# A one-core language-model layer: a new order table, extra identity turns on TensorE, and three smaller moves behind the attention

## Chip, core and metric

The kernel runs on one core of a Trainium2 chip. The metric is device time in microseconds (us) of one execution. Five engines work side by side and meet through semaphores: TensorE (PE in the profile, PEld its weight loads), VectorE (DVE), ScalarE (ACT), GpSimd (POOL) and SyncE (SP, which here only issues DMAs).

## What is computed

Ids of 4 x 512 tokens are hashed into an embedding table (192 wide), layer-normed, and pass through one attention block and one mixture-of-experts block.

```
h = layernorm_affine(table rows of the ids)            # 2048 tokens x 192
h = h + attention(layernorm(h))                        # 12 heads of 16
#   attn = softmax(q k^T / 4);  out = (attn v) W + b
#   t = out / |out| by head;  sim = softmax(10 t t^T where >= 0)
#   result = (sim v) W + b
h = h + moe(layernorm(h))                              # 8 experts, top 2
#   y = gelu(x w1[e] + b1[e]) w2[e] + b2[e], weighted, added by token
```

## The kernel before

**Attention.** The four sequences ("blocks" 0 to 3) have three groups of four heads each, 12 groups in all. For each group TensorE makes 16 score tiles of 128x512 three times: `max_unit` (row maxima, read by VectorE), `exp_unit` (scores again, ScalarE takes the exponential) and `sim_unit` (the second attention; ScalarE takes the exponential, VectorE's `mask` clears what stands under one). `pv` multiplies by V into an accumulator, ScalarE's `save` copies it out, TensorE's `normalise` turns it by transposes, and VectorE divides. `o_transpose`, `proj_norm` and `proj_out` are the projections behind it. All of TensorE's results pass through a ring of six PSUM banks. `wait_consumed(k)` waits until bank user k was read.

**The order.** `schedule()` lists all steps. The table `PLACE` gives each kind of step its positions in one common order `EVENTS`. Each engine walks this one list and takes the steps that are its own, so the table sets the order of work of each engine, SP's and GpSimd's DMA issues too. It holds no times.

**Routing.** While the last sequence is in its second attention, the first 12 token tiles are routed: VectorE's `shift`, `choose`, `place`, `mark` and `rows0` to `rows2` (24 one-hot tiles, one after another), TensorE's `list0` to `list2` (24 narrow matmuls, one for each one-hot tile), VectorE's `finish` (writes `slot_token`, from which GpSimd gathers expert inputs), and `share`, which works out the weights of the two chosen experts. The last four tiles ("late") are routed inside the expert loop.

**Behind the attention.** TensorE runs `o_transpose` and `proj_out` of the last sequence. VectorE adds into H, makes `out_norm` and X2. TensorE turns gathered tokens (`turn`), runs the first expert layer of a block of 128 slots (`first_wide`, 12 instructions, then `first_narrow`), turns X2 for the gate (`turn_gate`, `late_gate`), and goes into the loop `over_pairs`: 39 blocks, two by two. `second_layer(j)` waits for the GELU of block j and, before this change, for `y_weighted` of block j-2. VectorE's `weigh_output` adds the bias into Y, waits for the scatters of earlier blocks to land, and multiplies by the weight. GpSimd scatters Y with an adding DMA. In its second, fourth and sixth call (blocks 1, 3 and 5) `weigh_output` does the late routing between bias and weight. Weights w2 are loaded by eight DMAs that SP issues once `normalise` of the last group has been turned.

`keep_clock(bank, n)` multiplies the identity by the identity n times into a bank that nobody reads; 50 of these turns (`MASK_TURNS`) stand ahead of `pv` of the last group's third tile already.

Of the kernel before, what the change touches and what calls it, by code (L numbers as in the profile page):

```python
# [32 lines left out]
CT = N // P  # L33
# [29 lines left out]
MASK_TURNS = 50  # L63
PEELED = EARLY
# [10 lines left out]
def schedule():  # L75
# [43 lines left out]
    for t, part in ((0, "shift"), (0.1, "exp"), (2, "choose"), (4.5, "count"), (6, "place"), (7.5, "mark"), (7.7, "tag"),  # L119
                    (10.6, "rows0"), (10.8, "rows1"), (11, "rows2"), (12, "list0"), (12.5, "list1"), (13, "list2"),  # L120
                    (14, "finish"), (14.2, "stage"), (19, "share")):
        at(e + t, 6, "route", part)
    at(GB * UG * (B - 1) + GB * UG + OFF_E + 7.9, 6, "route", "take")
    for g in range(NG):
# [30 lines left out]
        0, 10, 60, 179),  # L155
    ('embed_norm', 'moments'): (
        1, 16, 65, 207),
    ('embed_norm', 'rstd'): (
        2, 27, 72, 231),
    ('embed_norm', 'centre'): (  # L160
        3, 34, 82, 233),
    ('load_qk',): (
# [4 lines left out]
    ('embed_norm', 'affine'): (  # L167
        7, 37, 91, 245),
    ('attn_stats', 'stats'): (
        8, 38, 96, 260),  # L170
    ('attn_stats', 'moments'): (
        9, 41, 108, 266),
    ('attn_stats', 'rstd'): (
        11, 44, 148, 272),
    ('attn_norm',): (
        13, 45, 175, 341),
    ('x_transpose',): (
        14, 18, 53, 64, 205, 212, 350, 353),
    ('q_proj',): (
        24, 67, 218, 398),  # L180
    ('mid', 'q_proj'): (
        26, 74, 224, 420),
    ('k_proj',): (
        33, 71, 222, 413),
    ('c_proj',): (
        35, 80, 234, 424),
    ('mid', 'k_proj'): (
        36, 78, 226, 422),
    ('v_proj',): (
        39, 43, 84, 92, 242, 249, 509, 521),  # L190
    ('mid', 'c_proj'): (
        40, 89, 241, 432),
    ('max_unit',): (
# [9 lines left out]
    ('max_row',): (  # L203
        70, 115, 164, 216, 268, 326, 389, 489, 557, 650, 734, 819),
    ('exp_unit',): (
# [109 lines left out]
def unit(kind, *args):  # L315

    return UNIT[(kind, args)]
# [1331 lines left out]
```

## Time and profile before

| | us |
|---|---|
| median of 3 runs | 600.11 (595.86 to 603.89) |
| the profiled execution, its own time | 599.07 |
| its span, first to last instruction | 597.3 |
| TensorE busy | 527.5 |
| VectorE busy | 428.8 |
| ScalarE busy | 336.5 |
| GpSimd busy | 226.8 |

### The profile page before, as it was taken

To read this page: it belongs to the slowest core of one execution; us is meant where nothing else is said; L and a number is where in the kernel's file an instruction comes from. 1 tells how busy PE (TensorE), PEld (TensorE's weight loads), DVE (VectorE), ACT (ScalarE), POOL (GpSimd) and SP (SyncE) were. 2 spreads that over 40 slices of the span, in tenths; PEclk is the share of its full clock that TensorE was granted. 3 is DMA by queue.
4 is the path that set the end of the run, shared out by engine and by line. 5 is a ranking of instruction groups with operands and counts; after the bars stand their busy time and mean duration, and the time that the engine had idled before them with its cause. 6 is when DMAs were issued, how large, how long until landed. Compare 5 with 4: busy or idle time off the path is not lost.

```text
span 597.3 us, 11968 instructions
## 1 busy us (share of the span) xinstructions
PE 527.5 (88%) x3532; PEld 322.8 (54%) x3533; DVE 428.8 (72%) x927; ACT 336.5 (56%) x790; POOL 226.8 (38%) x282
## 2 busy tenths in 40 slices
PE   0548899999999999999997987879999999999991
PEld 0223333443344323534253333568998999999990
DVE  3579997989898999897679999965775444434420
ACT  1223676768797888788977876215332424433430
POOL 6891221426151341102322320032455665656442
PEclk9979899999999999999998999868999999999996
DMA  4271142146442345321222659195232343333321
GB/s 118 61 128 32 37 72 45 41 69 115 52 71 56 57 67 76 42 66 47 63 49 86 87 115 289 43 314 189 33 52 44 57 62 49 47 60 47 45 29 20
DMA packets 42252, 45.24 MB, mean 76 GB/s; under 512 B 10419, under 2 KB 37045, under 8 KB 42198
## 3 DMA queue, kind: packets, MB, share of 16 engines
q0 software_dynamic: 12864, 19.97, 19.8%
q1 hardware_dynamic: 29334, 24.62, 18.0%
q8 instruction: 26, 0.43, 0.3%
q14 instruction: 28, 0.23, 0.2%
HBM read 17.88 MB, written 7.70 MB: 43 GB/s over the span
## 4 chain that ended last, share of the span: by engine, by line
PE 63%; DVE 19%; issue 6%; POOL 5%; ACT 3%; DMA 2%; DVEq 0%; POOLq 0%; ACTq 0%
PE psum L1400 12%; PE psum L1541 11%; PE psum L1518 8%; DVE MX L1187 6%; PE psum L1461 5%; PE psum L1468 5%; PE psum L1453 5%; PE psum L1525 4%; PE psum L1490 4%; DVE arena L1201 3%; POOL H L668 3%; PE psum L1425 2%; PE psum L1437 2%; ACT arena L828 2%; DMA result<-T,slot_dest 1%
## 5 line engine op out<-in xcount | busy, mean ns | idle before, releaser
L828 ACT ACTIVATE arena<-psum 128x512 f32<-128x512 f32 x384 | 205.1, 615 | 42.5 <-PE psum L1468 21.3
L1187 DVE TENSOR_REDUCE MX<-psum 128x1 f32<-128x512 f32 x192 | 123.3, 681 | 12.1 <-PE psum L1453 11.3
L1201 DVE SCALAR_TENSOR_TENSOR arena<-arena 128x1024 f32<-128x1024 f32 x96 | 117.1, 1241 | 10.3 <-ACT arena L828 10.1
L1400 PE MATMUL psum<-arena 128*17 128x512 f32 x768 | 102.9, 608 | 4.5 <-DVE arena L1201 3.1
L730 POOL DMA_INDIRECT result<-T,slot_dest x39 | 64.8, 1662 | 62.3 <-DVE T L1317 60.1
L573 POOL DMA_DIRECT2D KS<-arena x72 | 36.9, 514 | 112.1 <-PE psum L1468 53.7
L1468 PE MATMUL psum<-KS,QS 96*128 96x512 bf16 x192 | 66.3, 388 | 1.0 <-ACT arena L828 0.9
L712 POOL DMA_INDIRECT xg_sb<-x_rows,slot_token x39 | 40.1, 1028 | 69.4 <-DVE slot_token L1122 38.0
L861 ACT ACTIVATE arena<-psum,b_sb 128x128 f32<-128x128 f32 x120 | 32.2, 398 | 58.4 <-PE psum L1525 58.4
L1453 PE MATMUL psum<-late_stacks,arena 96*128 96x512 bf16 x144 | 51.6, 400 | 11.0 <-DMA late_stacks<-arena 7.6
L1518 PE MATMUL psum<-O,arena 128*128 128x128 f32 x468 | 58.9, 284 | 2.0 <-DVE O L942 1.3
L1518 PEld LDWEIGHTS psum<-O,arena 128*128 128x128 f32 x468 | 57.7, 200 | 2.8 <-DVE O L942 2.0
L573 POOL DMA_DIRECT2D late_stacks<-arena x72 | 37.1, 519 | 46.6 <-PE psum L1461 46.2
L1461 PE MATMUL psum<-arena,late_stacks 98*128 98x512 bf16 x144 | 52.5, 386 | 0.5 <-DVE MX L1187 0.3
L861 ACT ACTIVATE SQ<-psum,b_sb 128x128 f32<-128x128 f32 x60 | 16.6, 376 | 53.4 <-PE psum L1525 53.4
L564 POOL TENSOR_TENSOR arena<-arena 128x512 bf16<-128x512 f32 x18 | 21.7, 1210 | 64.2 <-ACT arena L780 64.2
L938 DVE COPY arena<-arena 128x1152 f32 x39 | 30.5, 798 | 19.5 <-PE psum L1525 12.6
L1317 DVE TENSOR_SCALAR T<-T,X 128x192 f32<-128x192 f32 x39 | 12.5, 320 | 43.9 <-DMA result<-T,slot_dest 32.1
L1468 PEld LDWEIGHTS psum<-KS,QS 96*128 96x128 bf16 x192 | 17.6, 99 | 46.4 <-issue 29.4
L1541 PE MATMUL psum<-arena 128*128 x240 | 41.1, 327 | 1.0 <-DVE T L1317 0.7
L1541 PEld LDWEIGHTS psum<-arena 128*128 128x128 f32 x240 | 38.7, 190 | 1.6 <-issue 1.5
L1461 PEld LDWEIGHTS psum<-arena,late_stacks 98*128 98x128 bf16 x144 | 13.9, 98 | 38.0 <-issue 17.0
(223 smaller groups left out, 759.7 us busy)
## 6 DMA issues: line engine op xcount, KB each, us to landing
late_stacks<-arena POOLq DMA_DIRECT2D x72, 64.0 KB, 3.7
QS<-arena SPq DMA_DIRECT2D x72, 64.0 KB, 3.6
KS<-arena POOLq DMA_DIRECT2D x72, 64.0 KB, 3.8
arena<-w SPq DMA_DIRECT2D x8, 576.0 KB, 9.3
arena<-arena SPq DMA_DIRECT2D x54, 64.0 KB, 3.6
arena<-w SPq DMA_DIRECT2D x8, 384.0 KB, 7.6
x_rows<-X SPq DMA_DIRECT2D x4, 384.0 KB, 3.9
result<-H SPq DMA_DIRECT2D x4, 384.0 KB, 5.0
```

Of the source, the lines that this page charges most:

```text
L573: eng.dma_start(dst[g % SLOTS[ps]][r * D:(r + 1) * D, :, :].rearrange("d h n -> d (h n)"), part_rows(role, parts[r], g)).then_inc(done[g % ...
L730: pool.indirect_dma_start(out, bass.IndirectOffsetOnAxis(ap=slot_dest[:, j:j + 1], axis=0), Y[j % 2], None, compute_op=ALU.add).then_inc(s ...
L828: act.activation((P1, P2)[ps][:, n % PRING, :], s, ACT.Exp, scale=(QSCALE, SIM_SCALE)[ps]).then_inc(done, 1)
L861: last = act.activation(HT[r][:, hc, :], hid_ps[h][hc], ACT.Gelu, bias=b1_sb[:, bass.ds(e, 1), hc:hc + 1].rearrange("p o h -> p (o h)"))
L1187: dve.tensor_reduce(MX[:, g % 2, CT * i + c:CT * i + c + 1], slot(k), AX_X, ALU.max).then_inc(freed[k % RING], 1)
L1201: dve.scalar_tensor_tensor(p, p, 1.0, p, ALU.is_ge, ALU.mult).then_inc(masked, 1)
L1400: last = pe.matmul(acc[ps][32 * i:32 * i + VW, :], V[b][:, c, GH * (g % GB) + i, :], (P1, P2)[ps][:, n % PRING, :], start=c == 0, stop=c = ...
L1453: last = pe.matmul(s, QS[0][sl][0:SD, i, c * P:(c + 1) * P], KS[0][sl][0:SD, i, :], start=True, stop=True)
L1461: last = pe.matmul(s, KS[0][sl][:, i, c * P:(c + 1) * P], QS[0][sl][:, i, :], start=True, stop=True)
L1468: last = pe.matmul(s, QS[1][sl][:, i, c * P:(c + 1) * P], KS[1][sl][:, i, :], start=True, stop=True)
L1518: pe.matmul(hid_ps[i][hc], W1S[i][:, hc * P:(hc + 1) * P], XGT[i][:, 0, :], start=hc % HB == 0, stop=False, skip_group_check=True)
L1541: last = pe.matmul(y_ps[i], HT[r][:, hc, :], w2_sb[:, bass.ds(e, 1), hc, :].rearrange("p o d -> p (o d)"), start=hc == 0, stop=hc == HC - 1)
```

## The change

1. `PLACE` is a new table. The order within the last stage, from the third-last group on, moves by a few places; of 789 steps of TensorE 270 change their position in its own order, nearly all by one to four.
2. `share` of the early tokens goes from the end of the list, ahead of `stage(1, 1)`, to behind `stage(2, 0)` in VectorE's program ("behind block 1's tokens").
3. `second_layer(j)` waits for `y_biased` of block j-2, no longer for `y_weighted`.
4. The last block (38) gets a Y buffer of its own, so its bias goes ahead of the wait for the scatter of block 36.
5. Identity turns: one ahead of every second list matmul (12), seven ahead of the last `pv`, seven ahead of the last `normalise`, three ahead of the last `o_transpose`, seven ahead of the last `proj_out`, and seven each ahead of and behind `turn(0, 0)`.

```
@@ schedule @@
-                    (14, "finish"), (14.2, "stage"), (19, "share")):
+                    (14, "finish"), (14.2, "stage")):
@@ PLACE (most of the table left out) @@
     ('embed_norm', 'affine'): (
-        7, 37, 91, 245),
+        4, 25, 98, 240),
...
     ('save', 1): (
-        465, 571, 656, 737, 818, 877, 944, 980, 1017, 1059, 1101, 1138),
+        464, 568, 656, 736, 817, 878, 944, 981, 1022, 1068, 1102, 1138),
...
     ('out_norm', 'rstd'): (
-        735, 932, 1062, 1147),
+        726, 936, 1062, 1147),
...
     ('route',): (
-        1088, 1092, 1106, 1117, 1118, 1120, 1125, 1129, 1131, 1132, 1134, 1135, 1136, 1137, 1139, 1146, 1149),
+        1088, 1091, 1106, 1116, 1118, 1120, 1125, 1129, 1131, 1132, 1134, 1135, 1136, 1137, 1139, 1145),
@@ buffers, GpSimd @@
-        Y = [T[:, 2 + i, :] for i in range(2)]
+        Y = [T[:, 2 + i, :] for i in range(2)] + [T[:, 0, :]]
-  ... Y[j % 2], None,
+  ... Y[2 if j == NBLK - 1 else j % 2], None,
@@ VectorE, weigh_output @@
+                    last = isinstance(j, int) and j == NBLK - 1
+                    y = Y[2 if last else i]
                     dve.wait_ge(y_filled, j + 1)
-                    wait_past(dve, scattered[i], 8 * j0)
-                    dve.tensor_tensor(Y[i], y_ps[i], ...).then_inc(y_biased, 1)
+                    if not last:
+                        wait_past(dve, scattered[i], 8 * j0)
+                    dve.tensor_tensor(y, y_ps[i], ...).then_inc(y_biased, 1)
                     dve.wait_ge(y_biased, j + 1)
+                    if last:
+                        dve.wait_ge(scattered[i], 16 * (j // 2))
@@ VectorE, before the loop @@
                 stage(2, 0)
+                share(0)
@@ TensorE (GAP_TURNS = 7) @@
                             if args[0] == "list0":
+                                wait_consumed(pe, k + 1 - RING)
                                 pe.wait_ge(tags_ready, 2)
                                 pe.wait_ge(row_ready, n * EARLY_TILES + t + 1)
+                                if t % 2 == 0:
+                                    keep_clock(slot(k + 1), 1)
                                 last = pe.matmul(tokens_ps, oh_row[n][:, t, :], ...)
+                        if (g, c, ps) == (NG - 1, CT - 1, 1):      # last pv
+                            wait_consumed(pe, k + 1 - RING)
+                            keep_clock(slot(k + 1), GAP_TURNS)
+                            if args == (B - 1, 1, 0):              # last o_transpose
+                                keep_clock(s, GAP_TURNS // 2)
+                        if args == (NG - 1, 1):                    # last normalise
+                            keep_clock(s, GAP_TURNS)
+                        if (kind, *args) == ("proj_out", B - 1, 0):
+                            keep_clock(s, GAP_TURNS)
@@ second_layer @@
-                    wait_past(pe, y_weighted, j - 1)
+                    wait_past(pe, y_biased, j - 1)
@@ behind the list of steps @@
                     pe.wait_ge(acc_saved[ps], NG)
+                keep_clock(gate_ps[1], GAP_TURNS)
                 pe.wait_ge(tokens_ready, 1)
                 pe.wait_ge(lists_ready, 1)
                 turn(0, 0)
+                keep_clock(gate_ps[1], GAP_TURNS)
```

## Rows read from the trace of the kernel before

**Rows 1.** Busy time by stretch: PE, PEld, DVE, ACT, POOL, then PEclk, DMA share, GB/s.

```profile
380.00:390.00 10.00, 7.84 (x77) 5.31 (x76) 9.64 (x41) 1.70 (x3) 0.00 (x0) 1.00 0.10 28
500.00:550.00 50.00, 50.00 (x438) 48.66 (x438) 20.22 (x45) 19.27 (x72) 30.87 (x23) 1.00 0.33 52
```

**Rows 2.** The same view, 1 us each, where the granted clock changes.

```profile
391.00:392.00 1.00, 0.57 (x2) 0.60 (x3) 0.21 (x1) 0.29 (x1) 0.70 (x2) 0.70 1.09 348
...
405.00:406.00 1.00, 0.76 (x7) 0.51 (x5) 0.56 (x2) 1.00 (x5) 0.00 (x0) 0.97 1.08 354
...
411.00:412.00 1.00, 0.38 (x4) 0.28 (x3) 0.96 (x5) 0.99 (x2) 0.82 (x1) 0.94 0.03 10
```

**Rows 3.** The chain that ended last, 383 to 412: start, duration, what.

```profile
384.89 3.90 DVE late_stacks L1109 x24
...
391.43 5.47 PE psum L1490 x16
...
399.50 2.93 PE psum L1518 x12
...
406.28 1.60 PE psum L1518 x12
...
411.75 4.54 PE psum L1518 x24
```

**Rows 4.** TensorE in order of time: start, duration, line, operands, count, idle before.

```profile
66.68 0.39 PE L1453 MATMUL psum<-late_stacks,arena 96*128 96x512 bf16 x1 [1.68 <-DVE MX L1187]
...
348.39 1.47 PE L1490 MATMUL psum<-PW,OT 97*128 97x192 f32 x8
...
377.27 5.86 PE L1362 MATMUL psum<-ident 128*128 128x128 f32 x50
...
384.94 1.05 PE L1400 MATMUL psum<-arena 128*17 128x512 f32 x8 [0.83 <-DVE arena L1201]
386.81 0.63 PE L1479 MATMUL psum<-ident,arena 128*128 128x128 f32 x4 [0.81 <-ACT arena L788]
387.27 1.77 PE L1375 MATMUL psum<-arena,late_stacks 128*128 128x32 bf16 x24
389.56 1.05 PE L1425 MATMUL psum<-ident,O 128*96 128x128 f32 x8 [0.52 <-DVE O L1212]
...
398.01 0.45 PE L1510 MATMUL psum<-ident,xg_sb 128*128 128x128 f32 x1 [1.12 <-issue]
...
450.00 2.21 PE L1541 MATMUL psum<-arena,X 128*128 x12 [1.34 <-DVE T L1317]
...
452.05 2.84 PE L1518 MATMUL psum<-O,arena 128*128 128x128 f32 x24
```

**Rows 5.** VectorE in order of time.

```profile
400.34 1.25 DVE L923 TENSOR_SCALAR X<-H,mv,rstd_out 128x192 f32<-128x192 f32 x4
...
410.67 0.19 DVE L1339 COPY LG<-psum 128x32 f32<-128x32 f32 x1 [1.96 <-PE psum L1577]
...
451.01 0.75 DVE L942 COPY O<-psum 128x256 f32<-128x256 f32 x2
...
585.46 0.36 DVE L1308 TENSOR_TENSOR T<-psum,arena 128x192 f32<-128x192 f32 x1 [2.09 <-DMA result<-T,slot_dest]
586.66 0.32 DVE L1317 TENSOR_SCALAR T<-T,X 128x192 f32<-128x192 f32 x1 [0.85 <-DVE T L1308]
```

**Rows 6.** Busy time by stretch where VectorE runs `share` (columns of Rows 1).

```profile
401.50:403.90 2.40, 2.40 (x17) 2.00 (x15) 2.02 (x12) 0.00 (x0) 0.00 (x0) 0.50 1.12 334
```

**Rows 7.** First gather of expert inputs: issue on GpSimd, then time to landing.

```profile
390.19 1.05 POOL L712 DMA_INDIRECT xg_sb<-x_rows,slot_token  x1 [37.96 <-DVE slot_token L1122]
...
DMA to landing us min/median/max: 6.6/6.6/6.6
```

**Rows 8.** The eight loads of w2 on SP: durations, first and last start, landing.

```profile
L646 SPq DMA_DIRECT2D arena<-w x8: 373/1458/2490, 387.5 to 396.3; - x8
...
DMA to landing us min/median/max: 4.1/9.3/11.0
```

More of the change, by code:

```diff
@@ L63 @@
 MASK_TURNS = 50
+GAP_TURNS = 7
 PEELED = EARLY
@@ L154 @@
     ('embed_norm', 'stats'): (
-        0, 10, 60, 179),
+        0, 8, 59, 191),
     ('embed_norm', 'moments'): (
-        1, 16, 65, 207),
+        1, 11, 65, 212),
     ('embed_norm', 'rstd'): (
-        2, 27, 72, 231),
+        2, 12, 80, 230),
     ('embed_norm', 'centre'): (
-        3, 34, 82, 233),
-    ('load_qk',): (
[4 rows of a table removed]
-    ('embed_norm', 'affine'): (
-        7, 37, 91, 245),
[L169 to L178, printed above, removed]
+        3, 13, 82, 233),
+    ('embed_norm', 'affine'): (
+        4, 25, 98, 240),
+    ('attn_stats', 'stats'): (
+        5, 31, 103, 263),
+    ('attn_stats', 'moments'): (
+        6, 34, 123, 272),
+    ('attn_stats', 'rstd'): (
+        7, 35, 135, 285),
+    ('attn_norm',): (
+        9, 39, 169, 339),
+    ('x_transpose',): (
+        10, 14, 51, 60, 206, 211, 351, 353),
@@ L179 @@
+    ('load_qk',): (
[4 rows of a table added]
     ('q_proj',): (
-        24, 67, 218, 398),
+        17, 66, 218, 400),
     ('mid', 'q_proj'): (
-        26, 74, 224, 420),
+        19, 72, 224, 419),
     ('k_proj',): (
-        33, 71, 222, 413),
+        21, 71, 222, 410),
     ('c_proj',): (
-        35, 80, 234, 424),
+        23, 78, 234, 428),
     ('mid', 'k_proj'): (
-        36, 78, 226, 422),
+        26, 76, 226, 421),
+    ('mid', 'c_proj'): (
+        30, 87, 243, 430),
     ('v_proj',): (
-        39, 43, 84, 92, 242, 249, 509, 521),
@@ L191 @@
-    ('mid', 'c_proj'): (
-        40, 89, 241, 432),
+        37, 38, 84, 91, 237, 245, 509, 521),
     ('max_unit',): (
[9 rows of a table removed]
[9 rows of a table added]
     ('max_row',): (
-        70, 115, 164, 216, 268, 326, 389, 489, 557, 650, 734, 819),
+        70, 112, 162, 215, 268, 325, 390, 492, 560, 651, 733, 820),
     ('exp_unit',): (
[9 rows of a table removed]
[9 rows of a table added]
     ('pv', 0): (
[3 rows of a table removed]
[3 rows of a table added]
     ('save', 0): (
-        142, 191, 243, 298, 361, 439, 534, 614, 705, 782, 860, 915),
+        142, 188, 244, 296, 359, 439, 531, 626, 702, 781, 856, 911),
     ('normalise', 0): (
-        159, 198, 250, 312, 370, 446, 540, 631, 711, 803, 875, 917),
+        161, 199, 251, 313, 369, 446, 543, 632, 714, 803, 879, 917),
@@ L729, in _ @@
                     pool.wait_ge(y_weighted, j + 1)
-                    pool.indirect_dma_start(out, bass.IndirectOffsetOnAxis(ap=slot_dest[:, j:j + 1], axis=0), Y[j % 2], None,
+                    pool.indirect_dma_start(out, bass.IndirectOffsetOnAxis(ap=slot_dest[:, j:j + 1], axis=0), Y[2 if j == NBLK - 1 else j % 2], None,
                                             compute_op=ALU.add).then_inc(scattered[j % 2], 16)
@@ L1112, in _ @@
                             stage(0, 0)
-                        elif part == "share":
-                            share(0)
                         elif part == "take":
@@ L1304, in weigh_output @@
                 def weigh_output(j0, j, i, meanwhile=None):
+                    last = isinstance(j, int) and j == NBLK - 1
+                    y = Y[2 if last else i]
                     e = dve.value_load(blk_expert[0:1, bass.ds(j, 1)], min_val=0, max_val=E - 1)
                     dve.wait_ge(y_filled, j + 1)
[L1307 to L1308 removed]
+                    if not last:
+                        wait_past(dve, scattered[i], 8 * j0)
+                    dve.tensor_tensor(y, y_ps[i], b2_b[:, bass.ds(e, 1), :].rearrange("p o d -> p (o d)"), ALU.add).then_inc(y_biased, 1)
                     dve.wait_ge(y_biased, j + 1)
+                    if last:
+                        dve.wait_ge(scattered[i], 16 * (j // 2))
                     if meanwhile is not None:
@@ L1386, in _ @@
                         if (g, c, ps) == (NG - 1, CT - 2, 1):
-                            wait_consumed(pe, unit("normalise", NG - 1, 1) - RING)
-                            keep_clock(slot(unit("normalise", NG - 1, 1)), MASK_TURNS)
+                            wait_consumed(pe, k + 1 - RING)
+                            keep_clock(slot(k + 1), MASK_TURNS)
+                        if (g, c, ps) == (NG - 1, CT - 1, 1):
+                            wait_consumed(pe, k + 1 - RING)
+                            keep_clock(slot(k + 1), GAP_TURNS)
                         if ps == 0:
```

33 lines of the change are left out of this document (16 added, 17 removed), and 94 rows, old and new, of the table PLACE.

## Prediction

> **What bounds the kernel now.** I read the busy time by stretch first, for the clock and for the engine that is never idle, then the chain of waits, then TensorE and VectorE in order of time around each wait that the change touches. Three stretches come out. In the expert loop TensorE is the bound: busy 50.00 of 50 us, clock 1.00 [rows 1]. In the attention TensorE and VectorE share the chain, and the waits are short. Between them, from 384 to 412 us, neither is full: TensorE is busy 7.84 of the ten us from 380 [rows 1], and the chain goes from VectorE's one-hot tiles to `proj_out`, `out_norm`, and the first expert block [rows 3].
>
> In that third stretch the reader is to look at the clock. It falls at about 391.3, comes back just ahead of 405.0, and falls again close to the end of the slice from 411 [rows 2]. What TensorE did before the first fall was short work with waits between (0.83, 0.81, 0.52 us) and 24 list matmuls of 32 columns, and `proj_out` came next [rows 4]. The price stands in pairs of rows. The 16 instructions of `proj_out` took 5.47 us at 1.2 GHz [rows 3], and eight of the same kind 1.47 at 2.4 GHz [rows 4]. `first_wide` took 2.93 us for 12 at 1.2 GHz and 1.60 for 12 at 2.4 [rows 3]. After the second fall, 24 took 4.54 [rows 3], against 2.84 at full clock [rows 4]. So much for what the turns are after. By what they cost, one turn is 5.86 / 50 = 0.117 us [rows 4] at full clock.
>
> **Do turns hold the clock?** The 50 turns ran alone from 377.27 to 383.13 [rows 4], and the clock was 1.00 through the ten us from 380 [rows 1] and on to 391.3 [rows 2]. So they count as work by the trace. The Trainium skill, page "TensorE: Matmul & The Clock Gate", section "Part 4: PE-mode transpose", says the opposite: in transpose mode the full clock doesn't engage, since it isn't counted as a busy TensorE in the same way. By that rule the new turns are only cost; by the trace of before it doesn't hold here. It is the third case below. What the trace can't show is how many turns are enough.
>
> **The turns, followed in time.** Nothing changes up to the last `pv` but the table. Seven turns are 0.82 us and stand in the wait of 0.83 ahead of the last `pv`, and the next seven in the wait of 0.81 ahead of `normalise` [rows 4]: nothing for both.
>
> The 12 turns among the list matmuls are not hidden. VectorE made the 24 tiles from 384.89 in 3.90 us, 0.163 each [rows 3], so 14 lie ready when the lists start at 387.27, and TensorE works them off at 1.77 / 24 = 0.074 each [rows 4]. With a turn for each two, a pair takes 0.265, still under VectorE's 0.326, so TensorE lags to the end: 24 x 0.074 + 12 x 0.117 = 3.2 us, the lists end at 390.45, against 389.04. That is 1.4 us on two paths. First, three turns (0.35) and `o_transpose` follow: it starts at 390.8, not 389.56 [rows 4], 1.2 late. The seven turns ahead of `proj_out` fit its wait for ScalarE's copy (0.82, from the end of `o_transpose` to 391.43, rows above). So `proj_out` starts at 392.65 and takes two times about 1.43 = 2.85 at full clock: it ends at 395.5, against 396.9, **1.4 early**. Second, `finish` has its lists 1.4 later, so the first gather goes out at about 391.6, not 390.19, and lands 6.6 later [rows 7], at 398.2. Before, it landed at 396.8 and `turn(0, 0)` at 398.01 [rows 4] waited for other things. It now becomes the late one: VectorE's add and statistics are done by 397.3, the seven turns ahead of `turn(0, 0)` (ready at 396.0, done by 397) are hidden by the gather, and the turn, its copy and the first `first_wide` come at 398.2, 398.5 and 398.9, against 399.50 [rows 3]: **0.6 early**. The seven turns behind `turn(0, 0)` lie in the wait for that copy.
>
> Because the copy now goes ahead of the moments, and waits for the gather, X2 (done at 401.6 before [rows 5]) comes some 0.4 later, at 402.0. `first_wide` and `first_narrow` of block 0 at full clock are done by 401.4, so `turn_gate` waits for X2, and ends at about 403.2 with `turn(1, 1)`. `first_wide` of block 1 starts at 403.8, against 406.28 [rows 3], **2.5 early**. From there to the first wide layer of block 2 was 411.75 - 406.28 = 5.47 us at full clock [rows 3], and stays that, if VectorE follows.
>
> **`share`.** It takes 2.02 us of VectorE and some 2.3 with its gaps, from 401.50 to 403.83 [rows 6]. Before, it was covered by TensorE at half clock. With TensorE 2.5 early it would have been on the path in its old place (`stage(1, 1)`, then the copy of block 1's tokens). In the new place it falls into the idle 1.96 us in which VectorE waits for the late gate [rows 5]: 2.3 - 1.96 = 0.35 sticks out. So the loop begins 2.5 - 0.4 = **2.1 early**, at 409.65. The eight w2 loads are the transfer that could cap this. The last was issued at 396.3 and landed within 11.0 [rows 8], at 407.3 counted from its start: 2.3 us of slack.
>
> **The second fall** has its own price: 4.54 - 2.84 = 1.7 us. No turns stand in the stretch ahead of it (`late_gate` with 8 columns at a time). Its work doesn't change, but where it lies does, and ahead of it TensorE now runs at full clock and almost without a gap. I take it as avoided in the likelier case, since the fall came so near the end of that stretch, and price the other separately.
>
> **`y_biased`.** `second_layer(7)` waited 1.34 us until 450.00 for the weighing of block 5 [rows 4], behind `share` and the tags of the late tokens. That wait goes. What is late next is VectorE itself: the copies of blocks 8 and on for TensorE come out of its queue only behind that weighing, the first at 451.43 (451.01 and half of 0.75, plus the semaphore) [rows 5], while `first_wide` started at 452.05 [rows 4]. So **0.6** comes back, not 1.34. The chain of VectorE and scatter landings from 424 to 450 doesn't change.
>
> **Last block.** Its bias waited 2.09 us for block 36's scatter, ran at 585.46, and the product followed at 586.66 [rows 5]. Now the bias is done before, and the product follows the landing (about 585.4) by one register load and a semaphore, some 0.4: 585.8. **0.85** saved, all on the end. GpSimd's scatter only follows.
>
> **The table.** Start to 42 us: the first maxima wait for GpSimd's queue of loads, which the new order leaves alone up to group 0's last load; `mid` of `c_proj` goes eight places up on GpSimd, ahead of loads of group 1, which are used only after group 0's maxima. ScalarE's root of sequence 1 now goes ahead of the second `x_transpose`, which delays the projections a little while the loads wait for GpSimd anyway: nothing. At 66.68 TensorE waited 1.68 us [rows 4] for VectorE, which had `embed_norm` of sequence 2 ahead of three maxima; these now come first. The wait is shortened, but VectorE does the same work in all. In the last stage `out_norm` of sequence 2 has its root ahead of `save` of group 9 and of three exponentials: X2 comes a little earlier, and the exponentials behind it a little later. Bounds from the rows: from -1.7 (that wait wholly gone, nothing else) to +1.7 (as much lost by a swap elsewhere). I take -1.0, nearer the gain, as that row shows a wait that the new order goes around and no row shows one that it makes.
>
> **Sum, likeliest case.** Turns and `share` 2.1, second fall avoided 1.7, `y_biased` 0.6, last block 0.85, table 1.0: 6.25. The profiled execution took 599.07 us (span 597.3 and 1.8 around it), 1.0 under the median. Against the mean of the four executions shown, 599.73, it gives 593.5; against the profiled one 592.8.
>
> **Cases.**
> A, 0.42: as summed, 593.5.
> B, 0.25: the clock holds over the first stretch and falls over the second. 1.7 less: 595.2. For it: no turns there, and 8-column matmuls. Against: the stretch is short.
> C, 0.13, the other side: the turns don't hold the clock, by the rule quoted from the Trainium skill or because they are too few. Place: between 391 and 405. Price: `o_transpose` 1.2 late; `proj_out` at half clock as before; the turns ahead of `turn(0, 0)` at 0.234 each, 1.64 us, and now in series: it runs 2.8 late; the seven behind it exceed the wait by 0.8: the expert block starts 3.6 late. Less 0.6, 0.85 and 1.0 from the rest: 1.15 slower, 600.9. It decides when the clock falls before 392.6, where `proj_out` starts. Against: the 50 turns.
> D, 0.08: the table loses. If ScalarE's earlier root stalls the exponentials of group 10 behind it for over a us, and the swap of maxima costs a new fall of the clock (1.7 by the second fall's rows), the table costs 3 in place of giving 1: 597.5.
> E, 0.12: the table gives more: the wait at 66.68 and the half clock behind it (2 x 1.7), and waits of the last stage: 5 in place of 1, so 589.5.
>
> **Range.** It reaches from 588 (E and some luck of the runs) to 600.5 (C less a little); the three runs of before alone spread by 8. 2%, 12 us, is about what a measurement of this kernel can tell from no change. Faster by more than that (under 588.1) only in part of E: 0.09. Slower: 0.01. The same: 0.90.
>
> **What would show it.** Right: PEclk 1.00 from 378 through 405; `proj_out` 16 instructions in about 2.9 us; lists ending 1.4 later against the one-hot tiles; `turn(0, 0)` ended by the gather; `first_wide` of block 8 released by VectorE's copy, no idle at `second_layer`; the last bias directly behind TensorE. Wrong: 0.50 in `proj_out` (C), 0.50 ahead of the loop (B), a loop start set by w2 (then the 2.1 shrinks), or the end of the attention moved by more than 2 us (D, E).

## The result, and the profile after

The changed kernel took 599.09 us (median of 20 executions, 597.97 to 602.92), the kernel before 597.57 (20, 595.78 to 603.89): ratio 1.0043, interval [1.0028, 1.0059]. So it was slower by some 2.6 us by the ratio, where 6.25 less had been summed. In two later groups of runs the same changed kernel came out at 0.9973 [0.9941, 1.0004] and 1.0006 [0.9984, 1.0027] (below). What follows finds a gain behind the attention and a new table that gives it back; why the three ratios differ is only in part explained. Two executions of table_alone_again (below), its profiled one among them, were slow ones, over 1.5% longer than its fastest, and are left out of its ratio.

The profiled execution took 602.92 us (span 601.1). By stretch, 396 to 410 us, columns as in [rows 1]; these answer to [rows 1, 2]:

```profile
396.00:397.00 1.00, 0.94 (x8) 0.73 (x7) 0.53 (x3) 0.56 (x2) 0.69 (x2) 1.00 1.10 341
401.00:402.00 1.00, 0.47 (x5) 0.23 (x3) 0.40 (x2) 0.00 (x0) 0.00 (x0) 1.00 1.02 326
402.00:403.00 1.00, 0.00 (x0) 0.00 (x0) 0.00 (x0) 0.00 (x0) 0.00 (x0) 0.68 1.05 328
409.00:410.00 1.00, 1.00 (x13) 0.88 (x10) 0.00 (x0) 0.32 (x2) 0.00 (x0) 0.91 1.10 338
504.00:554.00 50.00, 50.00 (x438) 48.66 (x438) 20.22 (x45) 19.21 (x72) 30.84 (x23) 1.00 0.33 52
```

The expert loop is as it was. The clock now holds through `proj_out` and falls at 402.4, in a slice in which no engine works at all. TensorE in order of time says what they wait for (answers to [rows 3, 4, 7]):

```profile
396.71 2.85 PE L1507 MATMUL psum<-PW,OT 97*128 97x192 f32 x16
400.51 0.96 PE L1367 MATMUL psum<-ident 128*128 128x128 f32 x7 [0.95 <-issue]
403.42 0.45 PE L1527 MATMUL psum<-ident,xg_sb 128*128 128x128 f32 x1 [1.95 <-DMA xg_sb<-x_rows,slot_token]
...
403.87 1.70 PE L1367 MATMUL psum<-ident 128*128 128x128 f32 x7
405.37 2.77 PE L1535 MATMUL psum<-O,arena 128*128 128x128 f32 x12
...
411.27 1.60 PE L1535 MATMUL psum<-O,arena 128*128 128x128 f32 x12 [0.52 <-DVE O L943]
...
417.30 2.92 PE L1535 MATMUL psum<-O,arena 128*128 128x128 f32 x24 [1.19 <-issue]
...
440.75 4.07 PE L1558 MATMUL psum<-arena 128*128 x24
444.78 2.94 PE L1535 MATMUL psum<-O,arena 128*128 128x128 f32 x24
...
449.68 2.12 PE L1558 MATMUL psum<-arena,SQ 128*128 x12
451.64 2.11 PE L1558 MATMUL psum<-arena,X 128*128 x12
...
455.18 2.94 PE L1535 MATMUL psum<-O,arena 128*128 128x128 f32 x24 [1.43 <-DVE O L943]
```

`proj_out` took 2.85 us, as forecast, against 5.47. But the first turn of gathered tokens waits 1.95 us for the gather and starts 7.9 us after its issue, where the landing alone took 6.6 before [rows 7]. The clock falls in that wait, the seven turns behind it take 1.70 us and not 0.96, and `first_wide` of block 0 takes 2.77 us, hardly less than the 2.93 of before [rows 3]. At the end, VectorE (answers to [rows 5]):

```profile
588.30 0.36 DVE L1310 TENSOR_TENSOR T<-psum,arena 128x192 f32<-128x192 f32 x1 [0.43 <-PE psum L1558]
590.47 0.32 DVE L1321 TENSOR_SCALAR T<-T,X 128x192 f32<-128x192 f32 x1 [1.81 <-DMA result<-T,slot_dest]
```

The bias no longer waits, as meant. The product waits for the scatter of block 36 instead.

And the one-hot tiles, which began at 384.89 [rows 3], began at 389.74: 4.9 us late, when of the new turns only the seven ahead of the last `pv` had run. Part of that lies at the start. VectorE, ScalarE and GpSimd of the changed kernel, in order of time:

```profile
23.23 7.37 POOL L675 MEMSET late_stacks<- 2x2048 bf16 x4
...
23.78 0.18 DVE L913 BATCH_NORM_AGGREGATE mv_x<-stats_in 128x2 f32<-128x6 f32 x1 [0.62 <-issue]
25.20 0.18 DVE L913 BATCH_NORM_AGGREGATE mv_x<-stats_in 128x2 f32<-128x6 f32 x1 [1.25 <-issue]
25.91 0.18 DVE L913 BATCH_NORM_AGGREGATE mv_x<-stats_in 128x2 f32<-128x6 f32 x1 [0.52 <-issue]
26.12 0.30 ACT L745 ACTIVATE log_in<-mv_x,eps_embed 128x4 f32<-128x4 f32 x1 [2.63 <-DVE mv_x L913]
26.57 0.57 ACT L799 ACTIVATE arena<-psum 96x512 f32<-96x512 f32 x1
```

The same in the kernel before:

```profile
21.77 0.21 DVE L912 BATCH_NORM_AGGREGATE mv_x<-stats_in 128x2 f32<-128x6 f32 x2
22.39 0.59 ACT L798 ACTIVATE arena<-psum 96x512 f32<-96x512 f32 x1 [0.26 <-PE psum L1425]
```

The copy that lets the projections start (L799, L798 before) now stands on ScalarE behind the root of sequence 1, the root waits for VectorE's aggregates, and these crept. The projections began at 27.24, not 23.08, and the first maxima at 44.41, not 41.92 (both starts from TensorE in order of time). Of these 4.2 us 1.4 lie ahead of that root already: the eight transposes of the first `x_transpose` steps, which began at 20.44, began at 21.81. What made the 2.5 us at the first maxima 4.9 by the one-hot tiles was not traced.

### The profile page after: what moved, and what is told of

Read it like the earlier page. It is cut to its first block, busy times and chain, and to the rows that moved or that the text cites. A ratio compares the mean times of both kernels' runs of the same rounds, so it can differ in the third digit from the quotient of the medians.

```text
span 601.1 us, 12066 instructions
## 1 busy us (share of the span) xinstructions
PE 531.6 (88%) x3582; PEld 325.1 (54%) x3583; DVE 431.3 (72%) x927; ACT 335.1 (56%) x790; POOL 228.6 (38%) x282
## 4 chain that ended last, share of the span: by engine, by line
PE 59%; DVE 21%; issue 6%; DMA 5%; ACT 4%; POOL 1%; DVEq 1%; POOLq 0%; ACTq 0%
PE psum L1411 10%; PE psum L1558 10%; DVE MX L1186 8%; PE psum L1535 7%; PE psum L1474 5%; PE psum L1481 4%; PE psum L1466 4%; PE psum L1542 4%; PE psum L1450 3%; PE psum L1507 3%; DVE arena L1200 3%; ACT arena L829 3%; DMA result<-T,slot_dest 3%; PE psum L1438 2%; PE psum L1367 2%
## 5 line engine op out<-in xcount | busy, mean ns | idle before, releaser
L1535 PE MATMUL psum<-O,arena 128*128 128x128 f32 x468 | 57.3, 279 | 3.1 <-DVE O L943 1.9
L1535 PEld LDWEIGHTS psum<-O,arena 128*128 128x128 f32 x468 | 56.0, 195 | 4.1 <-DVE O L943 2.7
L565 POOL TENSOR_TENSOR arena<-arena 128x512 bf16<-128x512 f32 x18 | 24.1, 1346 | 63.5 <-ACT arena L781 63.4
```

What stands on the lines that cost most here:

```text
L1535: pe.matmul(hid_ps[i][hc], W1S[i][:, hc * P:(hc + 1) * P], XGT[i][:, 0, :], start=hc % HB == 0, stop=False, skip_group_check=True)
```

## The experiments

The experiments ran in five groups, each on one chip with its own runs of the kernel before, so ratios are given, and medians in us. All differences are under 2%. In the traces I measured from T, the start of the first one-hot tile in VectorE's order of time (384.81 for the kernel before): it parts the attention from what the turns touch.

### The parts by themselves

**table_alone**: the kernel before with the new `PLACE` and nothing else (`share` right ahead of `stage(1, 1)`, as it was).

> The kernel before with the new table alone (share stays ahead of stage(1, 1)). Theory 1, the table loses: ScalarE's root of sequence 1 now stands ahead of the copy of the second x_transpose and waits for VectorE's moments, so q_proj starts later than 23.1 us in all executions, by 4 us in some; the whole is 2.5 to 4 us slower than the kernel before, 1.004 to 1.007. Theory 2, the turns lose and the table is free: ratio 0.998 to 1.001, and q_proj within 0.5 us of 23.1.

Measured 602.0, ratio 1.0063 [1.0038, 1.0088]. The projections started at 26.98, and T was at 387.81. The table costs.

**turns_alone**: the kernel before with the turns.

> The kernel before with the identity turns alone. Theory 1 (the table loses): the turns keep the clock through proj_out and give 0 to 1 us, since what they win there is lost again by a later first gather; ratio 0.998 to 1.001. Theory 2 (the turns lose): lists 1.4 us later, gather later still, and the loop starts 1 to 2 us later; ratio 1.002 to 1.004.

Measured 599.25, 1.0032 [1.0010, 1.0054]. `proj_out` took 2.85, and `first_wide` of block 0 1.52. Then, TensorE in order of time:

```profile
398.78 1.52 PE L1531 MATMUL psum<-O,arena 128*128 128x128 f32 x12
...
404.69 1.99 PE L1531 MATMUL psum<-O,arena 128*128 128x128 f32 x12 [2.29 <-DVE O L943]
```

With TensorE early, `share` in its old place stands ahead of VectorE's copy of block 1's tokens, and 2.29 us are lost, and the clock with them: these 12 took 1.99 us where they take 1.60 at full clock. So the loop began at T + 27.32, no earlier than the T + 26.94 of before, and with `share` moved as well (after_old_table, below) at T + 23.34.

**small_moves_alone**: old table, no turns; `share` moved, `y_biased`, the last block's buffer.

> The kernel before with share behind block 1's tokens, the wait on y_biased and the last block's own buffer; old table, no turns. Both theories: 0.6 us from y_biased and 0.1 to 0.85 from the last block, ratio 0.997 to 0.999. A third theory, that one of these moves is what loses, gives over 1.001.

Measured 596.81, 0.9978 [0.9951, 1.0006].

**after_old_table**: the changed kernel with the table of before.

> The changed kernel with the old table put back. Theory 1 (the table loses): faster than the kernel before by 1 to 3 us, 0.995 to 0.998, q_proj at 23.1 us. Theory 2 (the turns lose): 1.001 to 1.004, as slow as the changed kernel itself.

Measured 595.48, 0.9967 [0.9945, 0.9989]: below the kernel before, which ran beside it, and below the 599.09 of the changed kernel, measured apart.

### Is it the start?

**root_back**: the changed kernel, ScalarE's root of sequence 1 behind the copy again.

```
     ('embed_norm', 'rstd'): (
-        2, 12, 80, 230),
+        2, 19, 80, 230),     # places 13 to 19 go down by one
```

> The changed kernel, with one step of the new table moved: ScalarE's root of sequence 1 (embed_norm) back to its old place behind mid of q_proj. Theory 1a, the start is the whole of the table's loss: q_proj at 23.2 us instead of 27.2, one-hot tiles at 383 to 385.5, ratio to the kernel before 0.996 to 0.998, as the changed kernel with the old table (595.5 us). Theory 1b, the middle of the table loses as well: q_proj at 23.2 but the one-hot tiles at 386 or later, ratio 0.999 to 1.002. Rival: the late start is chance, and this run's q_proj may come at 27 too.

**memset_waits**: the changed kernel, with GpSimd's four memsets behind VectorE's moments.

```
+                pool.wait_ge(in_moments, 3)
                 for n in range(SLOTS[0]):
                     pool.memset(KS[0][n]...
```

> The changed kernel, with GpSimd's four memsets of the one rows held until the moments of sequence 1 are signalled. If these memsets (from 23.2 us) hold up VectorE's aggregates or their signal, ScalarE's root starts at 22 to 23.5 us and q_proj at 23 to 24. If the moments come late for another reason, the root stays at about 25.9, q_proj at 27, and the memsets start only behind it, so that the loads of keys (GpSimd's queue) come 2 to 3 us later as well.

Measured 596.92, 0.9998 [0.9978, 1.0017] (root_back), and 597.38, 0.9999 [0.9979, 1.0019] (memset_waits). The projections started at 23.00 and 23.27. I first took both for remedies. **changed_again** is the changed kernel as it stands, on another chip than these two:

> The changed kernel once more, for the profile of another execution: the 20 times so far fall into 13 at 598.0 to 599.7 us and 7 at 600.9 to 602.9, and the one profiled lay in the upper group. Theory 1 (the two groups are the start: aggregates into the memsets or not): if the profiled run is in the lower group, q_proj starts at 23 to 24.5 us in place of 27.2; if in the upper, again at about 27. Rival (the groups come from the clock's falls in the middle): a lower-group run with q_proj at 27.

Measured 595.59 (8 executions, 592.39 to 599.63), 0.9973 [0.9941, 1.0004], with the projections at 23.18 and no remedy in it. So the late start comes in some executions of the new table and not in others, and neither remedy was shown to do anything.

**table_root_back**: the new table alone, root put back.

> The kernel before with the new table alone, in which ScalarE's root of sequence 1 is moved back from place 12 to place 19, behind the second x_transpose and the middle of q_proj. Theory 1 (what table_alone lost is mostly the start: the copy of the second x_transpose stands behind a root that waits for VectorE's aggregates, and these come late beside GpSimd's gathers and memsets): q_proj starts at about 23.0 to 23.3 us and not at 27.0, no execution lies more than 3 us above the fastest, and the ratio to the kernel before falls from 1.0063 to 1.000 to 1.003. Rival (the new table loses in the middle of the attention and the start only shows it in some executions): the ratio stays at 1.005 or more with q_proj on time.

Measured 598.83, 1.0029 [1.0002, 1.0056], projections at 23.45; but its times still spread over 5.2 us, where theory 1 allowed 3. **root_forward**: w2_wait_late (the change with the old table and one wait of TensorE moved, below) with only that root put ahead of the copy (place 27 to 17).

> The kernel of w2_wait_late (old table) with one step moved the other way: ScalarE's root of sequence 1 goes from place 27 to place 17, ahead of the copy of the second x_transpose. Theory 1: the root is a gate whose price depends on when VectorE's aggregates end: where they end by 22.0 us the copy stays at 22.4 and nothing is lost, where they end 0.4 us later they run into GpSimd's memsets and q_proj starts 2 to 4 us late. So the times fall into two groups 2 to 4 us apart, or lie all in one of them: a ratio to the kernel before of 0.996 to 1.001, against 0.9942 of w2_wait_late. Rival (the root costs nothing by itself and it needs the rest of the new order, such as the earlier centring on VectorE): one group, ratio 0.994 to 0.995.

Measured 594.11, 0.9937 [0.9917, 0.9957], one group, against 0.9942 of w2_wait_late: with the old table the root costs nothing. The late start was in 3 of 7 profiles of the new table with its root in front (in two of them the aggregates ended in time, and VectorE and ScalarE both stood idle until 25.8), and in none of 10 of the old table. What the late start costs is not settled: T was at 385.75, 387.81 and 389.74 in the three profiles that have it, against 383.00 to 385.25 in the punctual ones of the changed kernel and its variants, and the profiled execution with 385.75 (moments_first, below) is the second fastest of 12. What makes VectorE stall there is not settled either. That aggregates ended 0.4 us late and ran into GpSimd's next gather was my theory, and moments_first (below) refuted it: its last one ended at 22.10, ahead of that gather at 22.25, and it stalled all the same.

### The same chip

With ratios of one kernel spread from 0.997 to 1.004 I had four measured side by side on one chip: **changed_third**, **old_table_again** (as after_old_table), **root_back_again**, **table_alone_again**.

> The changed kernel, on the same chip and in the same rounds as the other three of this call. It was 1.0043 the first time (20 executions, 597.97 to 602.92) and 0.9973 the second (8 executions, 592.39 to 599.63, q_proj on time at 23.18). Theory 1 (the start is a matter of 0.3 us in the landing of the first gathers: where VectorE's last aggregate of sequence 1 ends ahead of GpSimd's gather at 22.2 to 22.5 us nothing is lost, else ScalarE's root and the copy behind it come 3 to 4 us late): a median of 595.5 to 597.5 with few or no executions above 600 if the start is on time in the profile, 598.5 or more if q_proj is at 27. Rival (the second time was luck): 598 to 600 with q_proj on time.

> The changed kernel with the old table, again. The first time 0.9967. Theory 1 (the new table costs about 1 to 1.5 us in the middle even where the start is on time, seen in the one-hot tiles at 384.1 in place of 382.8): 1 to 2 us below changed_third. Rival (the new table costs nothing but the start): within 0.7 us of changed_third if that one has its start on time.

> The changed kernel with ScalarE's root of sequence 1 behind the second x_transpose, again. The first time 0.9998, on another chip than the changed kernel. Theory 1 (it only takes away the risk at the start): within 0.7 us of changed_third where that one has its start on time, 2 to 3 us below it where not. Rival (the place of the root matters apart from that): 1 us or more below changed_third with both on time.

> The kernel before with the new table alone, again. The first time 1.0063 with q_proj at 26.98. Theory 1: 1.002 to 1.004 with q_proj on time at 23.0 to 23.5, as table_root_back (1.0029), or again 1.005 or more with q_proj at 27. Rival (it is the table's middle that costs): 1.005 or more with q_proj on time.

| | median | ratio |
|---|---|---|
| changed_third | 597.94 | 1.0006 [0.9984, 1.0027] |
| root_back_again | 597.18 | 0.9992 [0.9969, 1.0015] |
| old_table_again | 594.60 | 0.9941 [0.9918, 0.9964] |
| table_alone_again | 599.42 | 1.0022 [0.9997, 1.0047] |

All four started the projections on time (23.18 to 23.32). The new table costs 3.3 us all the same (changed_third against old_table_again), more than either side had written, and root_back_again is within 0.8 of changed_third (0.7 had been allowed): the start isn't it. In the attention no loss shows: T was at 384.12 on average in the five profiles of the changed kernel and its variants with a punctual start (383.00 to 385.25), and at 384.13 in ten with the old table (382.67 to 385.56); by that spread, up to about 1 us could hide there (my estimate). The loss is behind T: from T to the last instruction these five took 211.2 us on average (210.1 to 212.4), after_old_table and old_table_again 207.9 and 208.7. TensorE and VectorE of changed_third, from T = 383.00:

```profile
396.79 0.30 PE L1527 MATMUL psum<-ident,xg_sb 128*128 128x128 f32 x1 [2.07 <-DMA xg_sb<-x_rows,slot_token]
397.04 1.69 PE L1367 MATMUL psum<-ident 128*128 128x128 f32 x7
397.27 0.42 DVE L943 COPY O<-psum 128x256 f32<-128x256 f32 x1 [2.62 <-PE psum L1528]
397.61 0.37 DVE L913 BATCH_NORM_AGGREGATE mv<-stats_out 128x2 f32<-128x6 f32 x4
398.52 2.42 PE L1535 MATMUL psum<-O,arena 128*128 128x128 f32 x12
403.56 1.60 PE L1535 MATMUL psum<-O,arena 128*128 128x128 f32 x12 [0.52 <-DVE O L943]
409.60 2.92 PE L1535 MATMUL psum<-O,arena 128*128 128x128 f32 x24 [1.19 <-issue]
```

and of old_table_again, from T = 385.05:

```profile
396.75 0.38 DVE L913 BATCH_NORM_AGGREGATE mv<-stats_out 128x2 f32<-128x6 f32 x4
397.21 0.30 PE L1527 MATMUL psum<-ident,xg_sb 128*128 128x128 f32 x1 [0.42 <-DMA xg_sb<-x_rows,slot_token]
397.46 0.93 PE L1367 MATMUL psum<-ident 128*128 128x128 f32 x7
398.22 1.52 PE L1535 MATMUL psum<-O,arena 128*128 128x128 f32 x12
402.36 1.60 PE L1535 MATMUL psum<-O,arena 128*128 128x128 f32 x12 [0.52 <-DVE O L943]
408.39 4.54 PE L1535 MATMUL psum<-O,arena 128*128 128x128 f32 x24 [1.18 <-DMA arena<-w]
```

Counted from T, the gather is issued at 5.80 in one and 5.81 in the other, and the first turn follows at 13.79 against 12.16: the gather is 1.6 us slower. The clock falls in the longer wait, so the seven turns behind it stick out by 0.7 us (1.69 against 0.93), and `first_wide` takes 0.9 more (2.42 against 1.52). The loop begins at T + 26.60 against 23.34, which is these three. In changed_third's own profile half of it comes back at the loop, whose first 24 matmuls take 2.92 us against 4.54; in changed_again, root_back and memset_waits they took 4.54 or 4.55, and nothing came back. One more difference: VectorE's copy of the gathered tokens stands ahead of the moments in the new table and behind them in the old.

**moments_first** takes that pair back out of the new table, **take_first** puts it alone into the old one:

```
     ('out_norm', 'moments'): (
-        721, 930, 1059, 1146),
+        721, 930, 1059, 1145),     # and route's last place from 1145 to 1146
```

> The changed kernel with one pair of neighbours in its table swapped back: moments of out_norm of the last sequence (place 1145) ahead of the copy of block 0's gathered tokens (take, place 1146), as in the old table. In the changed kernel VectorE stands idle for 2.6 us until the gather has landed and TensorE has turned the tokens, and only then makes the aggregates on which X2 and the late gate wait. Theory 1 (this swap is the table's cost): from the first one-hot tile to the loop's first_wide 23.4 us as with the old table, not 26.6; 2 to 3 us faster than the changed kernel, ratio 0.993 to 0.996. Theory 2 (the gather itself, 8.0 us from issue to turn(0, 0) in place of 6.35, is the cost and comes from the table elsewhere): 25 to 26 us, ratio 0.997 to 0.9995. Rival (the cost lies ahead of the one-hot tiles): ratio 1.000 or more.

> The changed kernel with the old table, and in it only that pair swapped: the copy of block 0's gathered tokens ahead of the moments of out_norm of the last sequence. Theory 1: the swap alone makes the old table as slow as the new one: 26 to 26.6 us from the first one-hot tile to the loop, ratio 0.999 to 1.001, against 0.994 to 0.997 of the old table. Theory 2 (the gather is late for another reason): the gather stays at 6.4 us, 24 to 24.8 us to the loop, ratio 0.996 to 0.998.

Measured 598.97, 1.0026 [1.0002, 1.0049] (its profile has the late start, 26.89), and 594.85, 0.9966 [0.9942, 0.9990]. From T the loop began at T + 26.24 and T + 23.75. The pair is worth 0.4 us each way, and the slow gather stays with the table (first turn at T + 13.77 and T + 12.22). Theory 2 holds: in the changed kernel the gather is the cost.

That is not what the table costs alone. In table_root_back and table_alone_again the gather landed in 6.4 and 6.6 us, as before, and yet their ratios were 1.0029 and 1.0022; T was at 384.38 and 387.03. What they lose was not traced.

What lies in the gather's way? The queues of DMA in the stretch from its issue to the turn, of changed_third (queue, kind: packets, MB, share of 16 engines):

```profile
q1 hardware_dynamic: 3065, 2.31, 93.9%
q0 software_dynamic: 126, 0.39, 14.6%
q8 instruction: 1, 0.02, 0.9%
```

and of old_table_again:

```profile
q1 hardware_dynamic: 2658, 1.99, 102.3%
q0 software_dynamic: 51, 0.14, 6.9%
```

One transfer of 16 KB of code stands out. Its record takes 1.15 us on one queue, against 0.04 for the mean packet of q1. In the packets of all 18 experiments and of both kernels it splits them without an exception: in the seven with new table and turns (first turn at T + 13.62 to 13.81) it starts 5.4 to 5.6 us after the gather's issue, while the gather's own packets move (in changed_third from 5.0 on); in all others at 9.0 or later (9.0 with the turns alone; with the new table alone 12.1 with the root back, and 13.2 and 13.9 as it was). The eighth load of w2 was held up in the same seven as well: its issue took 4.12 to 4.14 us there and 2.48 or 2.49 in the others that issue it at the same time from T (2.82 in lists_without_turns, where it comes some 2 us later). The seventh, which ends before the code transfer starts, took 1.78 to 1.93 in the seven and 1.72 or 1.73 in the old-table kernels with turns; the transfer can't explain that. SP's issues of w2 in changed_third:

```profile
L647 SPq DMA_DIRECT2D arena<-w x8: 373/1492/4122, 385.6 to 394.2; - x8
DMA to landing us min/median/max: 4.2/10.5/11.2
```

and in old_table_again:

```profile
L647 SPq DMA_DIRECT2D arena<-w x8: 373/1448/2477, 387.7 to 396.1; - x8
DMA to landing us min/median/max: 4.1/9.0/11.6
```

That is a coincidence in every profile, and it suggests the mechanism; a kernel that moves the code alone was not run, so the cause of the slow gather is argued and not shown. The Trainium skill, page "Runtime: NRT & Kernel Launch", section "Instruction fetch mechanics", has the sequencer fetch code in 16 KiB blocks by a DMA queue of its own, and calls the cost "mostly hidden". The size agrees, though the trace has code transfers of 8 KB as well. In 13 of these 20 profiles the transfer of 16 KB lay clear of the first gather, in seven it lay inside it.

### Around the lists and w2

These start from after_old_table. **w2_wait_late**:

```
-                pe.wait_ge(w2_in, 16 * E)
                 over_pairs(pe, step)
@@ second_layer @@
                     if isinstance(j, int) and j == 0:
+                        pe.wait_ge(w2_in, 16 * E)
```

> The changed kernel with the old table, and TensorE's wait for the w2 loads moved from ahead of the loop to ahead of second_layer(0). If the w2 loads set the start of the loop there (1.19 us of idle at 406.27, ended by that DMA), the loop's first_wide starts 1.2 us sooner against the one-hot tiles, and if the clock doesn't fall ahead of it another 1.7: 594.2 or 592.5 us, ratio 0.991 to 0.995. If the landing was hidden by the copy of tokens anyway, no change against 595.5.

Measured 593.41, 0.9942 [0.9919, 0.9964]: the same as old_table_again without it (0.9941). The loop began at T + 23.38 against 23.34, since VectorE's copy of tokens ends that wait now (1.15 us), where the w2 landing had (1.18).

**gather_first**: w2_wait_late, and SP starts the w2 loads only when `slot_token` is written, beside the first gather and not 3.2 us ahead of it:

```
                         sp.wait_ge(pv_done[0], CT * NG)
+                        sp.wait_ge(tokens_ready, 1)
                         for e in range(E):
                             sp.dma_start(w2_sb...
```

> As w2_wait_late, and SP issues the w2 loads only once the token list is ready, behind the first gather. If the first gather's 6.6 to 7.7 us come from standing in line behind w2, it lands within 3 to 4 us, TensorE doesn't wait for it at turn(0, 0), and that turn comes 0.5 us sooner; w2 lands 3 us later and may now be waited for at second_layer(0). 0 to 1 us faster than w2_wait_late. If the gather is slow by itself, nothing changes at turn(0, 0).

Measured 598.17, 1.0015 [0.9996, 1.0033]. The first turn came 6.08 us after the first gather's issue, against 6.44 in w2_wait_late, and the second and third gathers landed after 6.27 and 6.47 us against 6.75 and 6.83 (the trace has no landing of the first). So w2 ahead of it had held it up by 0.4 us, not by the 3 that I had thought possible. The price came elsewhere; VectorE and TensorE in order of time:

```profile
416.07 1.53 DVE L940 COPY arena<-arena 128x1152 f32 x2 [6.78 <-DMA arena<-b]
...
419.83 3.89 PE L1560 MATMUL psum<-arena 128*128 x12 [4.01 <-DVE rank L1006]
```

The load of the biases b2 (`arena<-b`) stands behind w2 on SP's queue, which issued it at 406.70 and not at 402.77; it landed 8.6 us later (6.8 in w2_wait_late), and VectorE, which waits for it ahead of the loop, and behind it TensorE, waited.

**lists_without_turns**: w2_wait_late without the 12 turns among the list matmuls.

> The kernel of w2_wait_late without the 12 turns among the list matmuls, all other turns kept. Theory 1 (the lists are on the path through the gather, and the 12 turns put the first gather 1.4 us later): the first gather is issued 4.4 us behind the first one-hot tile's start and not 5.8, turn(0, 0) comes about 1.2 us sooner unless something else holds it, and the clock stays up over proj_out because the seven turns ahead of it and the three ahead of o_transpose are enough: 0.5 to 1.2 us faster than w2_wait_late, ratio to the kernel before 0.992 to 0.9935. Rival (without them the clock falls in o_transpose or proj_out): proj_out takes 4 to 5.5 us in place of 2.85, the loop starts 1 to 2.5 us later, ratio 0.996 to 0.999.

Measured 593.92, 0.9950 [0.9909, 0.9992]. The clock held. The gather went out at T + 5.39, not 4.4 as I wrote, against 5.80: the 12 turns cost 0.4 us. (All five other kernels without these turns have 5.38 to 5.39 too.)

## Why the prediction was wrong

**The step that failed is the table**, the part "Start to 42 us ... nothing" and "I take -1.0". It read the new order by its places in the attention and put a price on swaps there; with the turns in, no sum of them shows (T at 384.12 and 384.13). Measured on one chip the table costs 3.3 us with a punctual start, and 1.3 to 3.8 as a whole when alone, where a gain of 1.0 was summed and a loss of 1.7 was the worst bound. Two things were missing.
- The start: "ScalarE's root of sequence 1 now goes ahead of the second `x_transpose`" was seen, and priced by where the root usually stands. It was a new wait of ScalarE for VectorE, and what is queued behind it is the copy on which TensorE's projections depend. The delay came only in 3 of 7 profiles, in the first of them 4.2 us at the projections and 2.5 at the first maxima. What it costs in the end is open, and so is what makes VectorE late.
- The gather: I took its 6.6 us from before, and made it the late one. It was, and was 1.6 slower. The profiles suggest, and no run shows, that a transfer that stood in nobody's way had moved into it. The 1.6 us became 3.3 at the loop: 0.7 in turns that ran at half clock on the path, which case C had priced at 0.8, and 0.9 in `first_wide`.

**Case D** had the right sign for the table (3 in place of -1) with another mechanism and ended at 597.5; it had 0.08. No case summed a late gather.

**Turns and clock: right in kind.** `proj_out` took 2.85 us to the digit, with the turns alone too. PEclk stayed 1.00 to 402.4 and not through 405. The rule in the Trainium skill, page "TensorE: Matmul & The Clock Gate", section "Part 4: PE-mode transpose", on which case C rested, doesn't hold here: by it the clock should have fallen ahead of `proj_out`. With the old table the loop began 3.6 us earlier than before from T (23.34 against 26.94), against 2.1 forecast: the list turns cost 0.4 and not 1.4, since a turn with its two list matmuls takes 0.20 us and not the 0.265 that I had added up, and the old table doesn't have the copy ahead of the moments (0.4).

**`share`: right**, in its sign and its reason; turns_alone shows what I wrote of its old place, and the price (2.29). In the new place TensorE waits 1.15 us for VectorE's copy behind it (w2_wait_late), 0.5 more than the 0.62 of before, for the 0.35 that was summed.

**The second fall: not avoided.** In the old-table kernels with turns the clock fell again at the loop: 4.40 to 4.57 us for 24. That is case B. In four of the seven kernels with new table and turns, the first profile of the changed kernel among them, these 24 took 2.92, as the clock had fallen and recovered just before; in the other three it fell both times (4.54 and 4.55). So the 1.7 was not gained in any of them without a fall ahead of it.

**`y_biased`: the wait went, the place of the gain was another.** There is no wait at `second_layer`, and the next `first_wide` waits 1.43 us for VectorE's copy, the one named. But from `second_layer(6)` to that `first_wide` it is 5.50 us (449.68 to 455.18), and was 5.51 before (446.54 to 452.05): the 0.6 of that place came to nothing, and to 0.1 in small_moves_alone and w2_wait_late. The gain lies one pair earlier, where I had written that the chain doesn't change. TensorE before, in order of time:

```profile
436.88 2.12 PE L1541 MATMUL psum<-arena 128*128 x12
439.69 2.21 PE L1541 MATMUL psum<-arena 128*128 x12 [0.69 <-DVE T L1317]
441.74 2.84 PE L1518 MATMUL psum<-O,arena 128*128 128x128 f32 x24
```

That is 4.86 us, and 4.03 after (440.75 to 444.78). So the size of 0.6 was about right by luck.

**Last block: right in kind, small in size.** The bias was free, and the product waits for the landing, as forecast. From the start of TensorE's last group of matmuls to the last scatter it was 5.37 to 5.57 us in the five kernels without this edit (5.57 before). With it, it was 4.76 to 4.97 in ten and 5.38 to 6.18 in five, the changed kernel's first profile (5.38) and old_table_again (6.18) among them: 0.35 less on average, for the 0.85. In old_table_again the product of block 36 had already waited 2.00 us for an earlier scatter, where it waited 0.68 before, and the saving went with it.

From loop start to the last scatter small_moves_alone took 174.11 us against 175.51 before: 1.4 for both edits, where 1.45 was summed. But 0.28 of that is the clock (its first 24 took 4.26 us), and old_table_again and changed_again, with the same edits, took 175.30 and 175.39. One pair of profiles doesn't show this sum.

**Sum.** Without its table the change is worth what case B says, or nearly: its 4.55 less the 1.0 of the table is 3.55 us, and 2.0 and 3.5 were measured (0.9967 and 0.9941). That the sum fits is partly luck, as terms missed to both sides. The table takes 3.3 of it back, measured side by side. Why the first comparison came out at 1.0043 and not near 1.0006 is open; its one profile had the late start.

The version that beats the kernel before is the change with the old table, with or without the later w2 wait: 0.9941 to 0.9967 in three comparisons whose intervals all lie below 1. Beside the changed kernel on one chip it was measured once, at 594.60 against 597.94.

## What to carry to other kernels

A reordering is priced at each place where an engine gets a new wait ahead of something that another engine needs, and the short stretch in which all engines wait for one transfer is where to look first. In a stretch that already hangs on one landing, list what else moves on the DMA engines, code included: in these 20 profiles one code transfer started anywhere from 5.4 to 13.9 us after the gather's issue, as instructions were added or moved. And take apart a bundle of edits before judging it: here four of five together were worth keeping (one of them, the turns, loses when alone), and the fifth hid them.

## What the runs showed that I had not expected

- The same kernel came to 1.0043, 0.9973 and 1.0006 of the kernel before in three groups of runs, the first with an interval apart from the other two. Its one profile was late at the start in the first and punctual in the others; only kernels measured side by side settled the cost of the table.
- In all seven profiles in which a 16 KB transfer of code fell into the first gather, that gather was slow (7.8 to 8.0 us from issue to use, against 6.35 in old_table_again). That the one causes the other was not tested.
- Identity turns in the waits kept TensorE at 2.4 GHz through `proj_out` (2.85 us against 5.47, turns_alone against before). Behind `proj_out` the clock held over 0.95 us of idle, seven turns and 0.42 us of idle (old_table_again), and fell where 1.95 us were left behind the seven.
- The first gather was only 0.4 us slower behind the start of the eight w2 loads (6.44 us from issue to use) than beside it (6.08).
